# Opening of a fused attention and mixture kernel: delta split and sent before the keys, query rows divided between two DMA queues

## What is computed

```python
qh = (q @ Wq.T + bq).reshape(B, L, H, E)      # q = layernorm(x)
kh = (k @ Wk.T + bk).reshape(B, S, H, E)      # k = v = context, S = 154
vh = (v @ Wv.T + bv).reshape(B, S, H, E)
scores = jnp.einsum('blhe,bshe->bhls', qh, kh)
scores = scores * tau[:, None, None, :] + delta[:, None, None, :]
a = jax.nn.softmax(scale * scores, axis=-1)
out = jnp.einsum('bhls,bshd->blhd', a, vh).reshape(B, L, D)
...
x = x + out @ Wo.T + bo
x = x + ffn(layernorm(x))                     # one of 8 experts for each token
```

## Time and profile before

| what | value |
|---|---|
| median of 3 runs | 412.96 us (412.38 to 413.06) |
| profiled execution, its own time | 413.04 us |
| its span | 411.2 us |
| PE busy | 380.7 us, 93% of the span |
| DVE busy | 258.4 us, 63% |
| ACT busy | 220.4 us, 54% |
| POOL busy | 140.2 us, 34% |
| mean granted PE clock | 0.967 of full speed |
| chain that ended last, share of PE | 77% |

### The profile page before, as it was taken

One profiled execution on the slowest core, in us unless ns is written; L12 is line 12 of the kernel. 1 busy time (PEld: TensorE's weight loads), 2 busy tenths in 40 slices (PEclk: granted clock), 3 DMA queues, 4 the chain that ended last, 5 costly groups with the idle time before them and its releaser, 6 DMA issues.

```text
span 411.2 us, 8873 instructions
## 1 busy us (share of the span) xinstructions
PE 380.7 (93%) x2907; PEld 263.1 (64%) x2912; DVE 258.4 (63%) x714; ACT 220.4 (54%) x433; POOL 140.2 (34%) x184
## 2 busy tenths in 40 slices
PE   7969999899999888978999999999999999999991
PEld 3545444456555444766776777887877778877680
DVE  3948985667777863886466634776556553665540
ACT  3314467656655566454555555666556565565540
POOL 5258150031011011367766431433511121155632
PEclk9979989999999999986999999999999999999996
DMA  7563769081101292134856562891039600001111
GB/s 222 127 185 75 146 141 274 6 181 52 50 26 53 84 376 72 63 109 139 313 189 219 152 225 62 301 383 48 27 97 421 175 27 28 0 34 60 38 65 38
DMA packets 29122, 54.33 MB, mean 132 GB/s; under 512 B 8482, under 2 KB 18774, under 8 KB 28950
## 3 DMA queue, kind: packets, MB, share of 16 engines
q1 hardware_dynamic: 25090, 45.72, 35.7%
q0 software_dynamic: 2688, 7.26, 5.5%
...
...
## 4 chain that ended last, share of the span: by engine, by line
PE 77%; DVE 7%; ACT 4%; issue 4%; SPq 3%; DMA 2%; POOL 1%; another core or an unknown queue 1%; ACTq 0%; DVEq 0%; POOLq 0%
PE bank L1342 22%; PE bank L1380 11%; PE bank L1334 8%; PE bank L1373 5%; PE bank L1064 4%; PE bank L1074 4%; PE bank L1156 4%; PE bank L1013 3%; PE bank L974 3%; PE bank L1052 2%; PE bank L1133 2%; ACT probs L1459 2%; DMA x_sb<-in_x_dram 2%; PE bank L1188 1%; DVE row_max L1729 1%
## 5 line engine op out<-in xcount | busy, mean ns | idle before, releaser
L1342 PEld LDWEIGHTS bank<-slot_rows,w_now 128*128 128x128 f32 x832 | 102.0, 194 | 6.2 <-issue 2.5
L1342 PE MATMUL bank<-slot_rows,w_now 128*128 128x128 f32 x832 | 103.5, 278 | 1.2 <-ACT slot_rows L1550 0.8
L1729 DVE TENSOR_REDUCE row_max<-bank 128x3 f32<-128x462 f32 (+1 forms) x96 | 53.5, 580 | 16.1 <-PE bank L1013 15.7
L2022 DVE SCALAR_TENSOR_TENSOR act_ut<-bank,b_of,gate 128x128 f32<-128x128 f32 x104 | 31.7, 346 | 49.7 <-ACT gate L1599 48.6
L1459 ACT ACTIVATE probs<-bank 128x512 f32<-128x512 f32 x80 | 45.8, 597 | 23.3 <-PE bank L1052 15.5
L1565 ACT ACTIVATE w_now<-w_sb 128x1024 f32 x52 | 54.7, 1054 | 2.7 <-DVE tile_expert L1955 2.1
L1380 PE MATMUL bank<-w_sb,act_ut 128*128 x208 | 54.8, 387 | 0.0
L1599 ACT ACTIVATE gate<-bank,b_of 128x128 f32<-128x128 f32 x104 | 32.3, 364 | 32.8 <-PE bank L1342 29.6
L1380 PEld LDWEIGHTS bank<-w_sb,act_ut 128*128 128x128 f32 x208 | 35.5, 190 | 15.5 <-issue 12.7
L755 POOL TENSOR_SCALAR var<-mv 128x1 f32<-128x1 f32 (+1 forms) x17 | 3.9, 232 | 110.2 <-DVE mv L1766 87.1
L881 POOL COPY piece_w<-w_sb 128x1024 f32 x24 | 25.1, 1057 | 45.1 <-PE bank L1334 43.4
...
...
## 6 DMA issues: line engine op xcount, KB each, us to landing
...
x_sb<-in_x_dram SPq DMA_DIRECT2D x4, 512.0 KB, 5.8
...
q_stack<-q_split ACTq DMA_DIRECT2D x6, 128.0 KB, 3.4
```

Of the source, the lines that this page charges most:

```text
L1342: ins = pe.matmul(h_ps[j % RING][:, P * m:P * (m + 1)], w1_now[:, whole_count(n) % 2, k, P * m:P * (m + 1)], slot_rows[:, tile_at(n), P * ...
L1729: dve.tensor_reduce(row_max[:, c % 2, m, t, first:first + k], score_bank(c, i)[:, 0:k * CTX].rearrange("p (h s) -> p h s", s=CTX), AX_X, A ...
L2022: ins = dve.scalar_tensor_tensor(act_ut[:, whole_count(n) % RING, m, :], h_ps[j % RING][:, P * m:P * (m + 1)], b1_of[:, q, tile_at(n), m:m ...
```

## The change

- On ACT, the DMA of delta moves from third to first place. 
- On DVE, the split of delta moves from between the two halves' query parts to the place ahead of `norm1(0)`.
- On SP, the store of delta, the rest of the constants, and both `load_d` stand ahead of `load_k(0)`. SP no longer issues query rows of half 0, and `load_second_half` issues the mid and low rows of half 1 after the keys. 
- On ACT, `load_first_q` issues all six rows of half 0, with waits for DVE's `first_mid` and `first_low`; the three high rows of half 1 go between the two copies of v.
- On PE, four matmuls of zeros stand ahead of the scores where fourteen stood.

```diff
-BUSY_BEFORE_SCORES, BUSY_FROM = 14, 4
+BUSY_BEFORE_SCORES, BUSY_FROM = 4, 4
...
-            def load_first_q(m):
+            def load_second_half():
 
                 for n, part in enumerate(Q_PARTS):
                     if part == 0:
                         continue
                     if n == Q_PARTS.index(1):
-                        sp.wait_ge(first_mid, m + 1)
+                        sp.wait_ge(first_mid, KD)
                     if n == Q_PARTS.index(2):
-                        sp.wait_ge(first_low, m + 1)
-                    sp.dma_start(q_rows(0, n)[:, m::KD, :], q_split[:, 0, m, part, :]).then_inc(first_q_loaded[m], 16)
+                        sp.wait_ge(first_low, KD)
+                    sp.dma_start(q_rows(0, n)[:, 1::KD, :], q_split[:, 0, 1, part, :]).then_inc(first_q_loaded[1], 16)
...
-            sp.wait_ge(pool_ready, 3)
-            load_k(0)
-            load_first_q(0)
             sp.wait_ge(d_split_done, 1)
             sp.dma_start(d_parts.rearrange("b w s -> b (w s)"),
                          delta_split[:, :, :].rearrange("b w s -> b (w s)")).then_inc(d_stored, 16)
-            load_first_q(1)
+            sp.dma_start(consts[:, FIRST_CONSTANTS:], const[:, FIRST_CONSTANTS:]).then_inc(s_consts, 16)
+            sp.wait_ge(pool_ready, 3)
             sp.wait_ge(d_stored, 16)
             load_d(0)
-            sp.dma_start(consts[:, FIRST_CONSTANTS:], const[:, FIRST_CONSTANTS:]).then_inc(s_consts, 16)
+            load_d(1)
+            load_k(0)
+            load_second_half()
             load_x(2)
-            load_d(1)
...
-            def load_first_high(m, pairs):
+            def load_first_q(m, pairs):
 
                 act.wait_ge(q_high, m + 1)
                 for n, part in enumerate(Q_PARTS):
                     if n in pairs:
+                        if n == Q_PARTS.index(1):
+                            act.wait_ge(first_mid, m + 1)
+                        if n == Q_PARTS.index(2):
+                            act.wait_ge(first_low, m + 1)
                         act.dma_start(q_stack[n:SPLIT:PAIRS, stack_slot(0), m::KD, :],
-                                      q_split[:, 0, m, 0, :]).then_inc(first_q_loaded[m], 16)
+                                      q_split[:, 0, m, part, :]).then_inc(first_q_loaded[m], 16)
...
-            load_first_high(0, (0,))
+            load_first_q(0, (0,))
             q_highs(0, 1)
-            load_first_high(0, (1, 2))
-            load_first_high(1, (0, 1, 2))
+            load_first_q(0, (1, 2, 3, 4, 5))
             for b in range(BATCH):
                 act.wait_ge(v_ready, b + 1)
                 act.activation(v_tmp[:, b, :, :].rearrange("p w n -> p (w n)"), st_ps[b][:, :],
                                ACT.Copy).then_inc(v_copied, 1)
+                if b == 0:
+                    load_first_q(1, (0, 1, 2))
...
             stats1_of(0)
+            dve.wait_ge(s_delta, 16)
+            split3(delta_sb[:, :], delta_rest[:, :], delta_split[:, 0, :], delta_split[:, 1, :], delta_split[:, 2, :],
+                   d_split_done)
             norm1(0)
...
             rest_of_first_q(0)
-            dve.wait_ge(s_delta, 16)
-            split3(delta_sb[:, :], delta_rest[:, :], delta_split[:, 0, :], delta_split[:, 1, :], delta_split[:, 2, :],
-                   d_split_done)
             rest_of_first_q(1)
```

2 lines of the change are left out of this document (1 added, 1 removed).

## The result

The changed kernel takes 410.72 us (median of 20 runs, 409.13 to 413.64), the kernel before 412.71 in the same comparison (20 runs). The ratio is 0.9965 with a 95% interval of 0.9951 to 0.9979, so a gain of 1.4 us, between 0.9 and 2.0; the two medians lie 2.0 us apart. The forecast was 407.7 with a range of 406.0 to 410.0: the direction was right, the size was not, and the time lies just above the range.

What follows compares the result with a forecast made beforehand. PE was taken as the bound once it has data, its late start and low clock setting the end. Gains of 3.8 and 2.2 us made PE's 6.0; min(6.0, DVE's 5.3) gave 413.04 - 5.3 = 407.7 us, range 406.0 to 410.0.

Steps and rivals of the forecast that it cites:

- Delta goes first: DVE ahead of the first normalisation: the 1.17 us split fits in 1.51 us of idle, costing 0.2 us (bounds 0 to 0.6).
- The store and its wait: SP ahead of the keys: store issued near 7.4, landing at 13.2 just behind bv; keys still start at 14.62, nothing lost.
- the store holds the keys: Rival on SP: store lands at 15.4, keys start 1.7 us later, about 409.2 us; chance 0.09, with a loss 0.03.
- The start of the scores: PE's first score matmul: 23.15 instead of 26.91, a gain of 3.8 us (bounds 3.1 to 5.7), released by a query row.
- Four zeros and the clock: PE ahead of the scores: zeros end at 20.7, 2.4 us of idle follow, and the clock holds.
- the price of 2.2 us: PE from first score to end of first projection: full clock takes 4.18 instead of 6.40 us, gaining 2.2.
- the clock falls in the gap: Rival on PE ahead of the scores: the 2.2 us are not gained, leaving 3.8, 409.2 us; chance 0.14.
- What is late next: DVE at chunk 2's statistics: x issued at 21.8, taken to land at 26.5; DVE through at 28.3, 3.6 us ahead.
- DVE's term: DVE's lead: 3.6 us at chunk 2's statistics plus 1.7 us of later idle filled, 5.3 us.
- PE's 6.0: PE's lead after the first projection: 3.8 us from the earlier scores plus 2.2 us from the clock.
- DVE decides more: Rival on DVE: x of chunk 2 lands at 28.0 or its idle does not fill; 3.5 to 4 gained, 409.3 us; chance 0.11.
- The end: From 36 us on PE is the chain almost without a break, so the 5.3 us gain carries to the end.

Runs made afterwards that it cites:

- e10: The kernel before with only delta's DMA moved to first place on ACT; 413.38 us, ratio 1.0033.
- e14: The changed kernel with delta's DMA third on ACT again and its split behind norm1(0); 410.00 us, ratio 0.9938.
- e7: e6, but SP waits until the keys have landed, then issues all six query rows of half 1, ACT none; 407.62 us, ratio 0.9869.
- e9: e7 with delta third on ACT, its split behind norm1(0), and x of chunk 2 ahead of SP's wait for the store; 407.04 us, ratio 0.9880.
- e8: The changed kernel with only delta's DMA moved back to third place on ACT; 410.82 us, ratio 0.9950.
- e13: e9 with fourteen matmuls of zeros ahead of the scores instead of four; 407.21 us, ratio 0.9866.
- e15: e13 without POOL's wait (its additions of bo no longer held until the first row maxima are split); 407.41 us, ratio 0.9869.
- e12: e9 without the wait for the keys, half 1's rows issued as in the changed kernel; 407.09 us, ratio 0.9880.
- e6: The changed kernel with x of chunk 2 ahead of the keys and POOL's additions of bo waiting for the first row-maxima split; 410.26 us, ratio 0.9935.
- e3: The changed kernel with POOL's additions of bo waiting until DVE has split the first row maxima; 410.28 us, ratio 0.9949.
- e5: The changed kernel with SP issuing x of chunk 2 ahead of the keys; 412.82 us, ratio 0.9911.
- e1: The changed kernel with SP waiting for x of chunk 1 before issuing the rest of the constants; 410.90 us, ratio 0.9971.
- e2: The changed kernel with fourteen matmuls of zeros ahead of the scores instead of four; 411.50 us, ratio 0.9986.

## Why the prediction was wrong, step by step

**Delta goes first: the first step that failed.** The prediction costed the DMA's move at 0 to 0.6 us of DVE's time, and looked only at delta, at the split and at bk, whose place it takes. The split did fit: the cast at 6.14, the first normalisation at 7.74, 0.1 us late, as forecast. What was not costed is that bk and tau, and with them most of what SP had under way, came later: bk 5.2 us after its issue instead of 3.9, ctx 7.3 instead of 5.9, bv 11.2 instead of 8.4, x of chunk 1 8.8 instead of 6.9. Nine profiles with delta third have x at 6.9 to 7.3 us, eight with delta first at 7.6 to 10.6. e10 prices the move by itself at 1.4 us, and e14 gets about 1.1 us back, at intervals that just touch; between e7 and e9 nothing of it is seen. For the store on SP the prediction asked which transfers it meets in the queue; for this move on ACT it did not ask which come later by it. Why one tiny transfer ahead of two others made of very small pieces does this is open. The runs show that it does, and that the constants don't.

**The store and its wait.** It cost nothing, as forecast, with a wide margin instead of a narrow one: issued at 7.31, it had landed by 11.14, when SP issued the broadcasts, while bv, issued ahead of it at 4.57, landed at 15.8. The value taken, 13.2, "just behind bv", was wrong. It came from the rule of ring order in the Trainium skill ("DMA: Bandwidth & Descriptors", Queues, rings and completion order), as I applied it. The same page of the Trainium skill, under Why a DMA increments its semaphore by 16 and not by 1, lets the number of DMA engines that a transfer uses depend on its outer dimension. By that this store of 2 partitions would use two, and bv's shares on the others could not hold it. The trace agrees in that the store landed by 11.14 and bv at 15.8; which DMA engines either used, no row shows. The rival in which the store holds the keys is out, though the keys were late, by another cause.

**The start of the scores.** Forecast 23.15, measured 25.11. The gain was 1.8 us instead of 3.8. The 2.0 us missing are the keys: issued 1.87 us late, and then landing 4.95 us after the last issue, where about 3.8 had been reckoned (18.0 to 21.8), which put them behind the query rows. No row stood behind that 3.8: the last key row landed after 4.0 to 5.7 us in every profile that shows it. With delta's DMA back in its place the start was 23.87 (e8) and 23.68 (e14), so 0.5 to 0.7 us late, and only in e8 was it a query row that released it. That e9 has 23.03 is partly luck: e13 and e15, which issue the same DMAs in the same order, have 23.83 and 23.88.

**Four zeros and the clock.** Forecast: idle 2.4 us, the clock holds. Measured: idle 2.95 us, and it fell. But the length of the idle stretch does not decide it alone. Around the first score the clock fell with an idle of 2.08 (e9), 2.14 (e8), 2.20 (e10), 2.58 (e14), 2.70 (e12), 2.95 (the changed kernel), 3.56 (e6) and 3.81 us (e3), and it held with 1.99 (e7), 2.34 (e5) and 3.10 us (e1). To read "holds for 2.4" out of one fall at 2.6 was too much; the traces would have borne an even chance at best. For PE alone the price of 2.2 us held: from the first score to the end of the first projection e1, at full clock, took 4.16 us, where 4.18 had been reckoned. In the changed kernel the clock was back at 29 us, and the stretch took 5.36 instead of 6.40, so 1.0 of the 2.2 was gained and PE was 2.8 us ahead there, not 6.0. What the low clock costs at the end was overrated: no loss is seen in the changed kernel (e1 and e2 gain nothing), where DVE waits for x, and 1.1 to 1.3 us of the stretch up to chunk 3 where it doesn't. The rival "the clock falls in the gap" described the trace, but its price was near zero here.

**What is late next: the term that was mis-sized.** The sum took DVE's term, 5.3, as the smaller one beside PE's 6.0; both were too large. DVE's term was 3.6 + 1.7. x of chunk 2 was to be issued at 21.8 and to land in 4.9 us, at 26.7. It was issued at 23.02, since the late keys stand ahead of it in SP's list, and took 6.3 us. The statistics started at 29.32 and were through at 31.15, so 0.8 us ahead of before, not 3.6. The idle that was to be filled did fill: from the start of these statistics to the cast of the row maxima DVE took 10.32 us before and 8.40 after, 1.9 us less where 1.7 was forecast, so at 37.72 DVE was 2.7 us ahead. Then came what the sum had no term for: coming earlier, the cast stood behind both of POOL's additions and took 4.22 us instead of 2.20. From the cast to the statistics of chunk 3 DVE took 13.26 instead of 12.07 us, 1.2 more. That leaves 1.5 us ahead at the statistics of chunk 3, and 2.0 at the end of the span. So of the 5.3 us, 2.8 went to the late x of chunk 2 and 1.2 to the cast. e5, which issues x of chunk 2 early and changes nothing else, gains 2.2 us over the changed kernel. The rival "DVE decides more" was the right one in kind, with a landing bound of 28.0 that was still 1.3 us short of 29.3.

**The end.** That a gain at the opening is carried through was right: the start of work on the first expert's weights moved from 185.06 to 183.20 us, by 1.9, and the span by 2.0; in e9 it moved by 5.1 and the span by 5.2.

In sum, the changed kernel gains 1.4 to 2.0 us of the forecast 5.3. With x of chunk 2 early and POOL's wait the same plan gains 1.2 to 1.3%, 4.9 to 5.5 us, with delta's DMA in its old place (e9, e12, e13, e15) and with it first (e7). These five kernels beat both the kernel before and the changed one and can't be told from one another.

**What stays open.** Why the order of three tiny DMAs moves a load of 512 KB, from 6.9 to 7.3 us to 7.6 to 10.6. A trace of it is seen one issue further on: SP's issue of bv took 0.84 to 0.99 us in the nine profiles with delta third and 1.12 to 2.44 in the eight with it first. Why delta's place costs 1.4 us in the kernel before and nothing that can be seen between e7 and e9. Why keys and rows land sooner in e7 than in e6; the profiles give 1.1 of the 2.7 us to the clock. What, beside the idle time, decides whether the clock falls. Whether the blocked cast's 1.2 us at chunk 3 reach the time: the comparisons show nothing beyond their uncertainty.
